# Linear attention and gated experts on one core: the DMA issues of the turned rows and keys change engines, and one batch's statistics change places

## The reference

```python
xn  = layernorm(x)                              # mean and variance over the 256 channels
q, k, v = split(xn @ wqkv); q, k = relu(q), relu(k)       # 16 heads of 16
num = q . cumsum(k v^T);  den = q . cumsum(k) + 1e-5      # along the sequence
attention = (num / den) @ wo
scores = sigmoid(xn @ Wr)                       # 8 experts, top 2 by scores + bias, normalised to cw
ffn = sum over 4 experts of cw * (silu(xn @ Wg) * (xn @ Wu)) @ Wd
ffn += (cw[4] + cw[6]) * xn + cw[7] * relu(xn) + causal depthwise convolution of xn, 4 taps
out = x + attention + ffn
```

## Time and profile before

| what | value |
|---|---|
| time, median of 3 runs | 1306.74 us (1305.68 to 1308.29) |
| time of the profiled execution | 1306.6 us |
| its span | 1304.5 us |
| PE busy | 1281.6 us, 98% of the span |
| VectorE busy | 1154.6 us, 89% |
| GpSimd busy | 831.4 us, 64% |
| ScalarE busy | 706.7 us, 54% |
| DMA engines, mean busy share of SyncE's queue and ScalarE's queue | 25.5% and 2.0% |

### The profile page before, as it was taken

The page is one execution under the profiler, slowest core; times in us unless marked ns, Lnnn a source line. Parts: engine busy times, 40 slices in busy tenths (PEclk is TensorE's granted clock), DMA queues, the critical chain, the costliest instruction groups (busy, mean ns, idle before and its releaser), DMA issues.

```text
span 1304.5 us, 56470 instructions
## 1 busy us (share of the span) xinstructions
PE 1281.6 (98%) x24036; PEld 1109.3 (85%) x24036; DVE 1154.6 (89%) x2748; ACT 706.7 (54%) x1487; POOL 831.4 (64%) x673
## 2 busy tenths in 40 slices
PE   5998999999999999999999999999999999999999
PEld 4887888888888888888888888888888888888887
DVE  7988898899988888988889988989888889889895
ACT  5635655456564556554565645655555555455552
POOL 2675666756667666667566676666675566766564
PEclk9999999999999999999999999999999999999999
DMA  5022222333223332223332233323233322232211
GB/s 185 4 75 80 70 73 55 89 85 79 62 58 85 88 83 71 72 55 89 85 86 56 59 85 88 84 70 72 55 91 85 85 55 74 69 89 69 69 41 37
DMA packets 247289, 96.74 MB, mean 74 GB/s; under 512 B 206976, under 2 KB 242688, under 8 KB 242944
## 3 DMA queue, kind: packets, MB, share of 16 engines
q1 hardware_dynamic: 214080, 88.44, 25.5%
q10 hardware_dynamic: 32960, 4.69, 2.0%
HBM read 53.18 MB, written 17.04 MB: 54 GB/s over the span
## 4 chain that ended last, share of the span: by engine, by line
PE 93%; DVE 4%; POOL 1%; issue 1%; DMA 0%; ACT 0%; DVEq 0%; POOLq 0%
PE ring L364 50%; PE scores L364 17%; PE ring L491 8%; PE ring L507 6%; PE scores L437 5%; PE state_sum L454 4%; PE ring L513 2%; PE scores L419 1%; DVE sm L966 1%; POOL hid L816 0%; DVE qks L941 0%; DVE ksum L933 0%; DMA x_t<-in_L_attn_x_dram 0%; POOL xl L797 0%; POOL xn L790 0%
## 5 line engine op out<-in xcount | busy, mean ns | idle before, releaser
L816 POOL TENSOR_TENSOR hid<-hid,cwb 128x512 f32<-128x512 f32 x128 | 165.8, 1295 | 186.8 <-DVE hid L998 176.7
L987 DVE SCALAR_TENSOR_TENSOR cT<-xT,conv_ws,cT 128x512 f32<-128x512 f32 x192 | 263.7, 1412 | 0.0
L804 POOL TENSOR_TENSOR x_t<-x_t,same 128x1024 f32<-128x1024 f32 x32 | 77.6, 2425 | 245.0 <-ACT same L660 245.0
L364 PE MATMUL ring<-xl,wgu_h 128*128 128x512 f32 x512 | 211.4, 413 | 0.0
L681 ACT ACTIVATE sg<-ring 128x512 f32<-128x512 f32 x128 | 76.7, 599 | 242.4 <-PE ring L364 242.3
L820 POOL TENSOR_TENSOR hl<-hid,hh 128x512 fp32r<-128x512 f32 x128 | 207.8, 1624 | 0.0
L364 PE MATMUL ring<-xh,wgu_h 128*128 128x512 f32 x512 | 201.1, 393 | 0.0
L364 PE MATMUL ring<-xh,wgu_l 128*128 128x512 f32 x512 | 200.7, 392 | 0.0
L599 ACT ACTIVATE yh<-yT 128x256 fp32r<-128x256 f32 x128 | 53.5, 418 | 237.3 <-DVE yT L1007 237.3
L973 DVE TENSOR_TENSOR state_bd<-state_sum,tables_s 128x256 f32<-128x256 f32 x248 | 104.2, 420 | 87.4 <-PE state_sum L454 80.9
L966 DVE TENSOR_TENSOR sm<-scores,causal_s 128x512 f32<-128x512 f32 x256 | 157.4, 673 | 2.1 <-PE scores L437 2.1
(11 more groups left out here) (135 smaller groups left out, 3489.9 us busy)
## 6 DMA issues: line engine op xcount, KB each, us to landing
cwb<-cw_rows SPq DMA_DIRECT2D x32, 1024.0 KB
x_t<-in_L_attn_x_dram SPq DMA_DIRECT2D x32, 512.0 KB
out_dram<-x_t SPq DMA_DIRECT2D x31, 512.0 KB, 3.3
xT<-qks_tok SPq DMA_DIRECT2D x672, 16.0 KB
ktok<-hid SPq DMA_DIRECT2D x496, 16.0 KB
xT<-qks_tok ACTq DMA_DIRECT2D x224, 16.0 KB
cw_rows<-cwt SPq DMA_DIRECT2D x128, 2.0 KB, 1.4
sm<-in_L_attn_wqkv_dram ACTq DMA_DIRECT2D x2, 384.0 KB, 5.2
```

The lines of the kernel that those rows point to most:

```text
L364: ins = mm(dst, lhs, rhs, start=first and n == 0, stop=final and n == len(passes) - 1, skip_group_check=not (first and final))
L804: pool.tensor_tensor(xb, xb, same[:, :, :], ALU.add).then_inc(s_base1, 1)
L816: pool.tensor_tensor(hid[:, e, :], hid[:, e, :], cwb[:, e, :], ALU.mult).then_inc(s_hid, 1)
L987: ins = dve.scalar_tensor_tensor(out=cT[:, c, :], in0=xT[:, third(s, j, 0), c, LEAD - HALO + n:LEAD - HALO + n + BT], scalar=conv_ws[:, c, ...
```

## The change

SyncE issues all 32 DMAs of the turned rows in one go, and ScalarE's eight go away. Of the keys' 16 DMAs SyncE issues two ahead of the spreading of `cw` (four before) and eight behind it (twelve before), and ScalarE issues the last six, behind `denominators` and so ahead of the next round's first table load and SiLU. Batch 3's statistics and normalising move from the middle of round 1 to where batch 4's stood, and batch 4's statistics move behind the last output addition of round 1, with its normalising last in GpSimd's round. In all later rounds the statistics stay where they are.

```diff
+    KEYS_SP = 10
...
                 if k:
-                    place_keys(s, j, k, range(1))
+                    place_keys(s, j, k, 0, 2)
                 sp.wait_ge(cw_out, at(s, j, 16 * P // BLK, (k + 1) * 16 * P // BLK))
...
                 if left > 1 and by_blocks(s, j, 2):
-                    place_turned(s, j, 2, 0, range(QUADS))
-                    place_turned(s, j, 2, 1, range(QUADS // 2))
+                    for c in range(C):
+                        place_turned(s, j, 2, c, range(QUADS))
                 if left:
                     spread_cw(s, j, 1)
-                    place_keys(s, j, 1, range(1, QUADS))
+                    place_keys(s, j, 1, 2, KEYS_SP)
...
-            def place_turned(s, j, n):
-
-                if n == 0:
-                    act.wait_ge(s_turn, at(s, j, 1, 3 - BY_PE))
-                    act.wait_ge(s_halo, at(s, j, 1, 1))
...
+            def place_keys(s, j, k):
+
+                act.wait_ge(s_kturn, at(s, j, 1, k))
+                for n in range(KEYS_SP, QUADS * QUADS):
+                    a, q = n // QUADS, n % QUADS
+                    act.dma_start(ktok[a * BLK:(a + 1) * BLK, 2:4, :, q * BLK:(q + 1) * BLK],
+                                  kb[q * BLK:(q + 1) * BLK, a, :, :, :]).then_inc(ktok_in, 16)
...
                     denominators(s, j, 1)
+                    place_keys(s, j, 1)
...
-                if by_blocks(s, j, 3) and not by_blocks(s, j, 2):
-                    normalise(s, j, 2)
                 weigh(1)
...
-                if left > 1 and not by_blocks(s, j, 3):
+                if left > 1 and not by_blocks(s, j, 2):
                     normalise(s, j, 2)
                 if left > 2 and by_blocks(s, j, 3):
                     normalise(s, j, 3)
...
                         mask(s, j, 0, 1)
-                        if by_blocks(s, j, 3) and not by_blocks(s, j, 2):
-
-                            statistics(s, j, 2)
...
-                if left > 1 and not by_blocks(s, j, 3):
+                if left > 1 and not by_blocks(s, j, 2):
                     statistics(s, j, 2)
                 elif left > 2:
                     statistics(s, j, 3)
...
                     dve.tensor_tensor(xb, done[:, 0:D], xb, ALU.add).then_inc(s_out, 1)
+                if by_blocks(s, j, 3) and not by_blocks(s, j, 2):
+
+                    statistics(s, j, 3)
```

More of the change, by code:

```diff
@@ L323, in place_turned, with place_keys @@
                                      xb_t[a * BLK:(a + 1) * BLK, c, q, :, :]).then_inc(xT_in[c], 16)
-            def place_keys(s, j, k, quarters):
+            def place_keys(s, j, k, first, stop):
                 sp.wait_ge(s_kturn, at(s, j, 1, k))
[L328 to L331, removed]
+                for n in range(first, stop):
+                    a, q = n // QUADS, n % QUADS
+                    sp.dma_start(ktok[a * BLK:(a + 1) * BLK, 2:4, :, q * BLK:(q + 1) * BLK],
+                                 kb[q * BLK:(q + 1) * BLK, a, :, :, :]).then_inc(ktok_in, 16)
             def batch(s, j, left):
@@ L711, in batch @@
                 high_y(0)
-                placing = left > 1 and by_blocks(s, j, 2)
                 silu(1)
-                if placing:
-                    place_turned(s, j, 0)
                 high_hid(0)
-                if placing:
-                    place_turned(s, j, 1)
                 high_y(1)
-                if placing:
-                    place_turned(s, j, 2)
                 if not last and not ahead:
@@ L724, in batch @@
                 silu(2)
-                if placing:
-                    place_turned(s, j, 3)
                 if not last and not ahead:
@@ L730, in batch @@
                 high_hid(1)
-                if placing:
-                    place_turned(s, j, 4)
                 high_y(2)
-                if placing:
-                    place_turned(s, j, 5)
                 silu(3)
-                if placing:
-                    place_turned(s, j, 6)
                 high_hid(2)
-                if placing:
-                    place_turned(s, j, 7)
                 high_y(3)
```

## The result

The changed kernel takes **1295.15 us** (median of 4 runs, 1294.63 to 1296.61), the kernel before 1306.97 in the same comparison: a ratio of 0.991, with a 95% interval of 0.9896 to 0.9924. It is 11.8 us faster, where 2.5 was forecast, and outside the range. The profiled execution took 1296.61 us with a span of 1294.8.

The account below looks back on a forecast made before the run. The prediction took TensorE, fully busy in settled rounds, as the bound. 4.6 us gained in round 1, 2.1 given back at the border and 0 from the DMA moves made 2.5 us less: 1304.2 us, range 1302.8 to 1308.0.

Parts of the forecast that it names:

- The premise: Settled rounds: TensorE is busy for all 39.90 us, so making another engine lighter shortens nothing.
- Part 4, the eight issues that ScalarE loses: Middle of settled rounds: ScalarE loses eight issues of 0.59 us where it waited anyway; effect 0.
- Part 4, the keys: Ahead of a round's first SiLU: ScalarE's six key issues leave it on time with 0.7 us left; cost 0.
- the rival of the late SiLU: Between `denominators` and the first SiLU: six key issues taking over 5.2 us delay it, costing 11 to 31 us; chance 0.12.
- Part 1: Round 1 without statistics in the middle: TensorE's idle time falls from 4.59 to 0.15 us, gaining 4.5 to 4.6 us.
- the three waits of the earlier trace: TensorE's idle time in round 1: 1.0 us for `state_bd`, 1.5 for the heads' sigmoid, 1.9 for the first output addition.
- Part 2: Border of rounds 1 and 2: batch 4's statistics placed there make TensorE idle for 2.1 us.
- the cheap border: Rival, border of rounds 1 and 2: VectorE arrives earlier, TensorE idles 1.5 us instead of 2.1, time 1303.6; chance 0.35.
- Part 3: Settled rounds: SyncE's 32 placing DMAs land with up to 1 us of VectorE wait, which is covered; cost 0.
- The rival that I named for "slower": The rival of the late SiLU: ScalarE's keys delay the round's first SiLU, time 1315 to 1335 us; chance 0.12.

Follow-up runs that it names:

- a2_dmas: The kernel before with all edits to the DMA issues and none to the statistics: 1299.12 us.
- a4_keys: The kernel before with only the keys split, ten on SyncE and six on ScalarE: 1307.41 us.
- a1_stats: The kernel before with the change's edits to `statistics` and `normalise` alone: 1302.50 us.
- a3_turned: The kernel before with only ScalarE's eight turned-row issues moved to SyncE, keys all kept on SyncE: 1361.14 us.

## Why the prediction was wrong

**The premise.** "Nothing that makes another engine lighter shortens a settled round" failed. It read PE's 39.90 busy of 39.90 us as 39.90 us of work. Busy counts a stretched burst in full, so the slowness stood inside the busy time and in no wait. The trace of before could have told: the same 128 instructions took 0.72 us in tile 0 and 0.87 to 0.93 in the tiles beside which two engines issue, and 0.72 in all four tiles of round 30, which places no rows.

**Part 4, the eight issues that ScalarE loses.** "ScalarE loses eight issues of 0.59 us in the middle, where it waited for PE or VectorE anyway: 0." The step costed the engine that issues and not its neighbours. a2_dmas puts this term, with the six keys, at 7.7 us, and a4_keys shows that the keys have no part in it. This is the term that broke the forecast. Of the 9.3 us by which the forecast missed, it is 7.7; the rest is the start, which gained more than the 2.5 us that were said.

**Part 4, the keys.** Nearly right in outcome, and by luck: the cover was thinner than said. The six issues took 4.55 us in round 14, not 3.8, the table load ended at 631.17 and the SiLU started at 631.28. The 0.7 us that was to be left is 0.1. Over the run the six took 3.9 to 5.4 us, 4.7 in the middle, with single issues up to 1.79 us where the sum took 0.63; in five rounds they went beyond the 5.2 us that the rival of the late SiLU named. That rival came about in part: in rounds 3 to 29 the SiLU started 0.2 to 1.2 us late in 11 of 27, and in six of these TensorE's burst followed late, by 1.6 us in all. Round 3 is the worst, ScalarE's two lines and the chain beside them:

```profile
156.17 1.28 ACT L680 ACT_TABLE_LOAD   x1 [5.11 <-issue]
157.46 0.60 ACT L680 ACTIVATE sg<-ring 128x512 f32<-128x512 f32 x1
...
157.60 0.56 issue
```

The step put this at 0. (By issues of 1.00 us its own sum overruns by 1.0 us, not 1.1.) Against the error of the forecast it is small, and a4_keys puts the keys' cost at nothing that can be told. The table load was 1.28 us and directly behind the last issue. The Trainium skill's 2.66 us for a switch ("ScalarE: Activation LUTs", "What ACT_TABLE_LOAD costs") would have ended 1.3 us after the SiLU's real start; no run here shows it.

**Part 1.** Right in kind: the three waits of the earlier trace rows are gone, and the long second product of L941 with them (the two take 1.29 us now). Round 1 keeps 0.41 us of idle, where 0.15 was said, and 0.33 of these are the start of the border.

**Part 2.** Right step by step. The statistics took 1.98 us to `state_bd` (2.00), GpSimd started 0.18 behind them (0.17), L773 came 1.11 later, and took 2.16. VectorE turned at 119.71, after 1.60 us of wait. TensorE idled for 0.33 and 1.25 us, 1.6 in all, which is nearer the 1.5 of the cheap border than the 2.1 of the sum. The rule of the Trainium skill ("SBUF — State Buffer", "Who interferes with whom") agrees with this trace: VectorE stood waiting, and GpSimd's four tiles took 2.16 us. Both parts together: a1_stats gained 3.4 us up to the first output addition of round 3, and 4.35 by the medians, where 2.5 was said.

**Part 3.** Right: 32 issues took 23.28 us (23.4 to 24.5 by the sum), the last landed 1.8 us from its issue (1.4 taken), VectorE didn't wait in round 14 and only once in the run, for 0.4 us. The lateness of `cw_rows` comes to 1.6 to 2.6 us by the sum's own times, where it says 2 to 2.6; from the first row's issue they started 1.4 us later than before. But "SyncE itself is late" was thought through for its DMAs and not for its sum. a3_turned shows how near the edge that was: eight more issues with the keys kept make SyncE's list 41.9 us on average and the kernel 54 us slower. The rival that I named for "slower" sat on ScalarE; the real danger of this edit was SyncE.

**Open.** How the two engines' DMAs slow TensorE's burst isn't settled. Shown are the moment (the last 0.7 us ahead of the burst; TensorE's program waits there for the tile's SiLU, which ends 0.7 us ahead of it), that it takes both engines, and that it doesn't take data. Whether SyncE's part is its issues or its transfers was not told apart, by which path they get in each other's way was not tried, and why 16 KB DMAs did less than tiny ones wasn't tried further.

## What to carry to other kernels

A busy engine may be slow and not only full: compare the same group of short instructions at several places of a round, beside quiet and beside busy neighbours, before writing that nothing else can shorten it. DMA issues are work for their queue, to be summed for a whole round against the bounding engine's time, and work next to bursts of small matmuls: keep two engines from issuing just ahead of one. Where DMAs move from one engine to another, move some back, and test the halves: here one half alone cost 54 us, over four times what the whole brings.

## What the runs showed of the hardware that wasn't expected

- DMA issues of ScalarE in the last 0.7 us ahead of a burst of 64 weight loads and 64 matmuls of 64 columns, while SyncE issues and moves its own, stretch it from 0.72 to 0.84 to 0.96 us; SyncE alone to 0.75 to 0.80, ScalarE alone to 0.76 at most.
- It doesn't take data for that: four DMAs of 4 bytes a round cost 11.5 us over the kernel, 4 us more than four of 16 KB at the same places.
- A burst can be stretched to 0.80 us of its 0.72 and cost nothing: the next tile's burst starts 4.71 us later either way.
- 28 semaphore updates by DMAs within a burst left it at 0.72 us.
- An issue of a 16 KB DMA takes a queue 0.60 us, and with its pauses 0.73 to 0.77: 32 in 23.28 us, six in 4.55; single ones took up to 2.1 us on SyncE and 1.79 on ScalarE.
